# Windowed attention: the second image's statistics move into the attention loop, the first image's pieces load ahead of the bias table

## The chip, the cores and the metric

One core of a Trainium2 chip. The metric is the time of one execution on the device, in microseconds; three runs of the kernel before gave 3354.16, 3354.45 and 3354.75 us, median 3354.45 us.

## The reference

The input x is (2, 128, 128, 128): 2 images, 128 channels, 128 x 128 pixels, float32.

```
x = x + attention(group_norm(x))       # 8 heads of 16 channels in windows of 16 x 16 pixels, with a bias table
x = x + deformable(group_norm(x))      # DCNv4, 3 x 3 kernel, 8 groups
group_norm(v): 32 groups of 4 channels; mean and variance over 4 x 128 x 128 values of one image
attention: softmax(q k^T * scale + bias[relative position]) v, then a projection
```

The attention's group norm needs, per image, the mean and variance of every channel over 16384 pixels before the first window of that image can be normalised. The change touches only these statistics and what is loaded around them.

## The kernel before, in words

Everything is written out by hand: each engine has its own instruction stream, and semaphores are the only order between them. `attention` is followed by `deformable` (the second residual block), which takes about the second half of the time and is not touched.

SP issues every DMA of `attention`, in program order, on one queue. Before the loop over windows it issues: three weight loads; 16 copies of the bias table into `rel_rows` in DRAM (L301); 16 loads of 1 MB of x into the two buffers of `stats_in` (L307: 8 pieces of 2048 pixels for image 0, then 8 for image 1, each waiting until the piece two before it was used); 16 loads that spread the bias table over `nbias` (L314); 6 chunks of four image rows into `strips` (L318), each waiting for the chunk two before it.

DVE computes `bn_stats` on each piece in four parts of 512 pixels (L638), then `bn_aggr` (L641) and the chain `group_scales` (L135 to L157) with a matrix multiply on PE (L451) that sums channels of a group, and a square root on ACT (L567). It does so for image 0 and then for image 1. After that it waits for `bias_in` and negates `nbias` (L651), and adds the bias of v for the first pair (`read_v`, L661).

POOL waits for the scales of both images (`gn_ready`), and for the chunks of strips that hold the first two windows. For each pair of windows it then copies them out of `strips` (L406), normalises them (L414), and after PE (L457, L461) and ACT (L575, L580) have made q and k it splits them into three bfloat16 parts (`split`, L423 to L432).

The attention works on 64 pairs of windows, 32 for each image. A pair has 16 slots, one for each head of each of its two windows. In slot n: PE computes the scores (L479) into one of two PSUM banks, which is free again when DVE has read the slot two before; DVE adds the bias and takes the row maximum (`bias_max`, L674, two instructions with a register read each); ACT takes the exponential (L587); PE transposes the probabilities of slot n - 2 (L492); DVE copies odd slots' transposes (L683) and ACT even ones (L594); PE multiplies by v after each fourth slot (`weigh`, L507). At slot 7 and slot 15 DVE normalises one finished window (`norm`, L689 and L694), at slot 9 it reads v of the next pair (L661). All engines hold the loop over pairs as a first pair, a loop with two pairs in its body, and three last pairs.

In each pair SP issues: a clearing store to `far_sums` (L354); the strip chunk for six pairs on (L361); `restack`, 12 loads of 128 KB into `stack` for the next pair (L344), which are to land before PE's slot 0 of that pair; the stores of the finished windows (L349); and, when POOL has split the pair after the next, the store of its parts (L330), which `restack` of the next round reads back. SP waits in between for what each needs; its pair ends with the store of the window that DVE normalises at slot 15.

Of the kernel before, what the change touches and what calls it, by code (L numbers as in the profile page):

```python
# [14 lines left out]
B, C, H, W = 2, 128, 128, 128  # L15
PIX = H * W
P = 128
# [20 lines left out]
AHEAD = 2  # L38
GN_EPS = 1e-5
CHUNK = 4 * W  # L40

# [132 lines left out]
def attention(nc, x, w_qkv, b_qkv, bv_row, rel_rev, attended, rel_rows, parts_dram, info_out, far_sums):  # L174


    with ExitStack() as ctx:
# [59 lines left out]
        bias_in = sem("bias_in")  # L237
        bias_neg = sem("bias_neg")
# [53 lines left out]
        def _(sp):  # L292
# [4 lines left out]

            for xq in range(WS):
                src = bass.AP(rel_rev.tensor, rel_rev.offset + WS - 1 - xq, [[REL, NH * REL], [1, WS]])
                dst = rel_rows[xq].rearrange("(r k) -> r k", k=WS)  # L300
                sp.dma_start(dst, src).then_inc(rows_out, 16)  # L301
            for b in range(B):
                for n in range(NSTAT):
                    i = b * NSTAT + n
                    if i >= 2:
                        sp.wait_ge(st_used, count(i - 1))
                    sp.dma_start(stats_in[:, i % 2, :], x_chan[b][:, n * 2048:(n + 1) * 2048]) \  # L307
                      .then_inc(st_in[i % 2], 16)
# [6 lines left out]
            for n in range(6):  # L315
                if n >= 2:
                    sp.wait_ge(chunk_in[n % 2], count(16 * (n // 2)))
                sp.dma_start(strips[:, n * CHUNK:(n + 1) * CHUNK],  # L318
                             x_chan[0][:, n * CHUNK:(n + 1) * CHUNK]).then_inc(chunk_in[n % 2], 16)
# [68 lines left out]
        def _(pool):  # L388
# [45 lines left out]
            pool.wait_ge(gn_ready, count(2 * B))  # L434
# [4 lines left out]
            with pool.Fori(0, (PAIRS - 2) // 2) as i:  # L439
                for par in range(2):  # L440
                    normalise(2 * i + 2 + par, par)
                    split(2 * i + 2 + par)

        @block.tensor
        def _(pe):
# [3 lines left out]
            for b in range(B):  # L449
                pe.wait_ge(gn_step, count(3 * b + 3))  # L450
                nc.tensor.matmul(x_ps[:, 0:2], gmat[:], ex[:], start=True, stop=True).then_inc(gn_sum, 1)  # L451

# [99 lines left out]
            with pe.Fori(0, (PAIRS - 4) // 2) as i:  # L552
                pair(2 * i + 1, 1)
                pair(2 * i + 2, 0)
            pair(PAIRS - 3, 1)
# [8 lines left out]
        def _(act):  # L564
            for b in range(B):
                act.wait_ge(gn_ready, count(2 * b + 1))
                nc.scalar.activation(gv[:, 1:2], gv[:, 0:1], ACT.Sqrt).then_inc(gn_root, 1)  # L567
            act.wait_ge(weights_in, count(48))
# [51 lines left out]
            with act.Fori(0, (PAIRS - 4) // 2) as i:  # L620
                pair(2 * i + 1)
                pair(2 * i + 2)
            pair(PAIRS - 3)
# [8 lines left out]
        def _(dve):  # L632
            for b in range(B):
                for n in range(NSTAT):
                    i = b * NSTAT + n
                    dve.wait_ge(st_in[i % 2], count(16 * (i // 2 + 1)))
                    for m in range(4):
                        ins = nc.vector.bn_stats(bn[:, 4 * n + m, :], stats_in[:, i % 2, m * 512:(m + 1) * 512])  # L638
                    ins.then_inc(st_used, 1)
                dve.wait_ge(st_used, count(NSTAT * (b + 1)))  # L640
# [6 lines left out]
                group_scales(nc, dve, x_ps[:, 0:2], gst, gv, gn[:, b, 0:1], gn[:, b, 1:2], recip_done, 9 * b,  # L647
                             gn_ready, 2 * b, gn_root, b)
            RB = 9 * B
# [35 lines left out]
            def norm(win, w, par, k):  # L685
# [5 lines left out]
                dve.wait_ge(recip_done, count(RB + win + 1))  # L691
# [7 lines left out]
            def pair(p, par, first=False, left=AHEAD):  # L699
# [14 lines left out]
            with dve.Fori(0, (PAIRS - 4) // 2) as i:  # L714
                pair(2 * i + 1, 1)
                pair(2 * i + 2, 0)
# [918 lines left out]
```

## Time and profile before

| what | value |
|---|---|
| median of 3 runs | 3354.45 us |
| profiled execution, its own time | 3350.4 us |
| span of its trace (first to last instruction) | 3348.7 us |
| busy: PE, DVE, ACT, POOL | 81%, 81%, 56%, 33% of the span |
| first scores of the attention | 129 us from the span's start |
| end of the attention | about 1560 us |

"Busy" counts the instructions that an engine executes, not waits or DMA issues. In a timeline row the first number is the start, the second the time that the row covers, then come the engine, the line of the kernel and the operation; xN says that N instructions are merged, and the bracket at the end gives the idle time before the row and what ended it. SPq is SP's queue of DMA issues. The page's chain of waits covers the deformable half of the span, so the first half is read from timelines.

### The profile page before, as it was taken

The page shows a single profiled execution, that of the slowest core. Times are in us where ns is not written, and L with a number is a line of the kernel's source. Part 1 is how long each engine was busy: PE and PEld are TensorE (multiplying, and loading weights), DVE is VectorE, ACT ScalarE, POOL GpSimd, SP SyncE. Part 2 cuts the span into 40 slices and gives each one's busy share as a digit, 9 for nine tenths or more (in the row PEclk, how much of TensorE's full clock was granted, in tenths as well). Part 3 has the DMA queues.
Part 4 walks back from the last instruction along what each step waited for, and adds up shares of the span by engine and source line. Part 5 has one row for each costly group of instructions (what it writes and reads, how often), then busy time and mean ns, then how long its engine had stood idle before and what let it go on. Part 6 is the DMA issues. An engine that isn't in the chain of part 4 may idle for free.

```text
span 3348.7 us, 78453 instructions
## 1 busy us (share of the span) xinstructions
PE 2717.4 (81%) x22424; PEld 2178.8 (65%) x22424; DVE 2716.9 (81%) x6553; ACT 1882.3 (56%) x3529; POOL 1102.7 (33%) x1525
## 2 busy tenths in 40 slices
PE   0599999999999999995665999897856699989886
PEld 0355655565556655563555888887845598888885
DVE  5488888888888888885656999998945599999996
ACT  0488888888888888885262444442204544434420
POOL 0333333333333333332415322135421241115550
PEclk9999999999999999998898999998978899999998
DMA  6788888888888888885642333233365333333334
GB/s 221 126 142 140 146 136 142 139 144 137 143 139 147 136 142 138 141 143 109 199 138 84 99 97 98 93 99 88 89 242 160 110 118 94 96 96 98 105 91 161
DMA packets 350617, 432.47 MB, mean 129 GB/s; under 512 B 42224, under 2 KB 275072, under 8 KB 344304
## 3 DMA queue, kind: packets, MB, share of 16 engines
q1 hardware_dynamic: 338544, 423.85, 56.5%
q0 software_dynamic: 11904, 6.44, 1.6%
q8 instruction: 97, 1.59, 0.2%
q14 instruction: 72, 0.59, 0.1%
HBM read 283.33 MB, written 147.09 MB: 129 GB/s over the span
## 4 chain that ended last, share of the span: by engine, by line
DVE 19%; DMA 8%; issue 8%; PE 6%; POOL 6%; POOLq 2%; DVEq 1%; ACT 1%; SPq 1%; ACTq 0%
DVE prod L1536 11%; DVE tt L1520 2%; PE sum_ps L1297 2%; DMA vring<-vals 2%; DMA vals<-vring 2%; DMA vring<-attended 2%; DVE x L1547 2%; POOL gath L1113 2%; POOLq L1120 1%; PE wt_ps L1275 1%; DMA o_sel<-off_out,pos 1%; DVE my L1515 1%; PE sum_ps L1237 1%; POOL i_sel L1113 1%; PE om_ps L1260 1%
## 5 line engine op out<-in xcount | busy, mean ns | idle before, releaser
L587 ACT ACTIVATE prob<-sbias,nmax 128x256 f32<-128x256 f32 x2048 | 905.0, 501 | 196.1 <-DVE nmax L674 194.1
L1536 DVE TENSOR_TENSOR prod<-vring,wt_ps 128x1920 f32<-128x1920 f32 (+3 forms) x512 | 902.7, 1816 | 58.9 <-DMA vring<-vals 49.2
L674 DVE CUSTOM_DVE_ANT_0 sbias<-s_ps,nbias 128x256 f32<-128x256 f32 x2048 | 766.9, 421 | 224.3 <-PE s_ps L479 211.8
L1297 PE MATMUL sum_ps<-d_ident,prod 128*128 128x128 f32 x6400 | 758.7, 276 | 23.5 <-DVE prod L1536 23.5
L492 PE MATMUL pt_ps<-a_ident,prob 128*128 128x128 f32 x4096 | 644.3, 280 | 134.1 <-ACT prob L587 131.6
L1297 PEld LDWEIGHTS sum_ps<-d_ident,prod 128*128 128x128 f32 x6400 | 721.4, 143 | 38.4 <-DVE prod L1536 31.6
L492 PEld LDWEIGHTS pt_ps<-a_ident,prob 128*128 128x128 f32 x4096 | 447.3, 140 | 277.6 <-DVE probT L683 118.4
L479 PE MATMUL s_ps<-stack 96*128 96x256 bf16 x2048 | 396.2, 274 | 9.5 <-DMA stack<-parts_dram 9.5
L683 DVE COPY probT<-pt_ps 128x512 f32<-128x512 f32 x512 | 351.7, 687 | 11.8 <-PE pt_ps L492 11.7
L423 POOL CAST parts<-qk 128x1024 bf16<-128x1024 f32 x64 | 66.3, 1036 | 860.1 <-ACT qk L580 860.1
L1403 ACT COPY ssum<-sum_ps 128x512 f32<-128x512 f32 x64 | 37.5, 586 | 513.6 <-PE sum_ps L1307 513.6
L1275 PE MATMUL wt_ps<-tt,d_ident 128*128 128x144 f32 x2304 | 312.0, 291 | 0.0
L1275 PEld LDWEIGHTS wt_ps<-tt,d_ident 128*128 128x128 f32 x2304 | 306.9, 195 | 0.9
L479 PEld LDWEIGHTS s_ps<-stack 96*128 96x128 bf16 x2048 | 174.8, 98 | 203.5 <-issue 137.0
L594 ACT COPY probT<-pt_ps 128x512 f32<-128x512 f32 x512 | 290.2, 567 | 0.0
L507 PE MATMUL o_ps<-probT,va 128*32 128x256 f32 x4096 | 274.1, 385 | 0.9 <-DVE probT L683 0.9
L1128 POOL COPY first_e<-first_at 128x2 f32 x16 | 2.8, 178 | 784.3 <-issue 784.3
L1390 ACT ACTIVATE hat<-off,one_col 128x576 f32<-128x576 f32 x128 | 140.5, 1098 | 198.2 <-DVE tt L1520 198.2
L1520 DVE TENSOR_TENSOR tt<-hat,my 128x864 f32<-128x864 f32 x192 | 192.4, 1057 | 9.1 <-PE wt_ps L1275 0.5
L674 DVE DVE_READ_ACCUMULATOR2_ANT nmax<- 128x1 f32 x2048 | 170.8, 83 | 0.0
L1381 ACT COPY off<-om_ps 128x864 f32<-128x864 f32 x64 | 56.3, 880 | 202.6 <-PE om_ps L1260 184.9
L507 PEld LDWEIGHTS o_ps<-probT,va 128*32 128x32 f32 x4096 | 106.9, 109 | 87.8 <-issue 33.9
(166 smaller groups left out, 3489.9 us busy)
## 6 DMA issues: line engine op xcount, KB each, us to landing
stack<-parts_dram SPq DMA_DIRECT2D x768, 128.0 KB, 7.4
vring<-vals SPq DMA_DIRECT2D x270, 320.0 KB
parts_dram<-parts SPq DMA_DIRECT2D x64, 768.0 KB, 6.5
off_out<-off SPq DMA_DIRECT2D x64, 432.0 KB
strips<-x SPq DMA_DIRECT2D x68, 256.0 KB, 3.6
a_stats_in<-x SPq DMA_DIRECT2D x16, 1024.0 KB, 4.9
far_sums<-nothing SPq DMA_DIRECT2D x64, 256.0 KB, 2.1
attended<-on SPq DMA_DIRECT2D x256, 64.0 KB
```

The source lines that it names most:

```text
L479: mm = nc.tensor.matmul(s_ps[:, n % 2, half, :], stack[:, par, 0, h, at:at + P], stack[:, par, 1, h, w * NT:(w + 1) * NT], start=True, sto ...
L492: mm = nc.tensor.transpose(pt_ps[:, T_BANK[n % 4], kh, half * P:(half + 1) * P], prob[:, n % 4, half, kh * P:(kh + 1) * P], ident[:])
L507: mm = nc.tensor.matmul(o_ps[32 * j:32 * j + VA, t * NT:(t + 1) * NT], va[:, par, 2 * w + kh, 4 * t + j, :], probT[:, (4 * k + j) % 8, kh, ...
L587: ins = nc.scalar.activation(prob[:, n % 4, half, :], sbias[:, n % SBIAS, half, :], ACT.Exp, bias=nmax[:, n % SBIAS, half:half + 1], scale ...
L594: nc.scalar.copy(probT[:, n % 8], pt_ps[:, T_BANK[n % 4]]).then_inc(t_read_a, 1)
L674: ins = nc.vector.tensor_tensor_reduce(out=sbias[:, n % SBIAS, half, :], in0=s_ps[:, n % 2, half, :], in1=nbias[:, h, half, :], scale=1.0, ...
L683: nc.vector.tensor_copy(probT[:, n % 8], pt_ps[:, T_BANK[n % 4]]).then_inc(t_read_v, 1)
L1275: mm = nc.tensor.matmul(acc[:, :, jx:jx + KS, jy * G:(jy + KS) * G], ident[:], tt[:, jx, jy, 2 * half:2 * half + 2].rearrange("p r (a k) - ...
L1297: mm = nc.tensor.matmul(sum_ps[:, par, r * H:(r + 1) * H], prod[:, r % 2, dx, dy * C:(dy + 1) * C], ident[:], start=(r + dx + dy == 0), st ...
L1390: nc.scalar.activation(xy(hat[:, j]), xy_off(s), ACT.Abs, bias=0.0 if j == 1 else one_col[:, j // 2:j // 2 + 1]).then_inc(dist_ready, 1)
L1520: ins = nc.vector.tensor_tensor(tt[:, jx], hat[:, jx, :, 0:KG].unsqueeze(1) .to_broadcast([P, 3, COLS, KG]), my[:], ALU.mult)
L1536: nc.vector.tensor_tensor(prod[:, r % 2, first:last].rearrange("p a (t c) -> p (a t) c", c=CG), vring[:, at:at + wide].rearrange("p a (t c ...
```

## The change

SP issues pieces 0 and 1 of image 0 ahead of the 16 bias table transfers, pieces 2 to 7 behind them, then the six strip chunks, and only then the 16 `nbias` loads. The 8 pieces of image 1 are no longer loaded there. Instead image 1 is cut into 16 pieces of 1024 pixels (512 KB), one for each of the pairs 1 to 16: SP issues the load at the start of its pair, and DVE takes `bn_stats` of the two halves after `bias_max` of slot 10 and of slot 12. Behind pair 16, DVE, PE and ACT run the chain of aggregation, group sums, square root and scales for image 1, and a second loop does pairs 17 to 60. POOL waits for image 0's scales at its start and for image 1's before pair 32. The semaphore of the chain's steps is a new one (`gn_coef`) in place of `recip_done`, and PE waits on it before it uses the bank again.

```diff
+STAT_PAIRS = 16
+STAT_AT = 10
+STAT = PIX // STAT_PAIRS
...
+            def load_stats(n):
+                if n >= 2:
+                    sp.wait_ge(st_used, count(n - 1))
+                sp.dma_start(stats_in[:, n % 2, :], x_chan[0][:, n * 2048:(n + 1) * 2048]).then_inc(st_in[n % 2], 16)
+
+            for n in range(2):
+                load_stats(n)
             for xq in range(WS):
...
-            for b in range(B):
-                for n in range(NSTAT):
...
+            for n in range(2, NSTAT):
+                load_stats(n)
+            for n in range(6):
+                if n >= 2:
+                    sp.wait_ge(chunk_in[n % 2], count(16 * (n // 2)))
+                sp.dma_start(strips[:, n * CHUNK:(n + 1) * CHUNK],
+                             x_chan[0][:, n * CHUNK:(n + 1) * CHUNK]).then_inc(chunk_in[n % 2], 16)
             sp.wait_ge(rows_out, count(16 * WS))
             for yq in range(WS):
...
-            for n in range(6):
...
-            def pair(p, par, first=False, left=AHEAD):
+            def pair(p, par, first=False, left=AHEAD, piece=None):
+                if piece is not None:
+                    sp.wait_ge(st_used, count(NSTAT - 1 + piece))
+                    sp.sem_inc(sp_passed, 1)
+                    sp.dma_start(stats_in[:, 1 - par, 0:STAT],
+                                 bass.AP(x.tensor, x.offset + C * PIX + piece * STAT, [[PIX, P], [1, STAT]])) \
+                      .then_inc(st_in[1 - par], 16)
...
-            with sp.Fori(0, (PAIRS - 4) // 2) as i:
-                pair(2 * i + 1, 1)
-                pair(2 * i + 2, 0)
+            with sp.Fori(0, STAT_PAIRS // 2) as i:
+                pair(2 * i + 1, 1, piece=2 * i)
+                pair(2 * i + 2, 0, piece=2 * i + 1)
+            with sp.Fori(0, (PAIRS - 4 - STAT_PAIRS) // 2) as i:
+                pair(2 * i + STAT_PAIRS + 1, 1)
+                pair(2 * i + STAT_PAIRS + 2, 0)
...
-            pool.wait_ge(gn_ready, count(2 * B))
+            pool.wait_ge(gn_ready, count(2))
...
+            pool.wait_ge(gn_ready, count(4))
...
+            def group_sums(b):
                 pe.wait_ge(gn_step, count(3 * b + 3))
                 nc.tensor.matmul(x_ps[:, 0:2], gmat[:], ex[:], start=True, stop=True).then_inc(gn_sum, 1)
+                pe.wait_ge(gn_coef, count(9 * b + 1))
...
+            def stat_piece(par, piece, half):
+                if half == 0:
+                    dve.wait_ge(st_in[1 - par], count(16 * (NSTAT // 2 + 1) + 16 * ((piece - (1 - par)) // 2)))
+                ins = nc.vector.bn_stats(bn[:, bass.ds(2 * piece + half, 1), :].rearrange("p a b -> p (a b)"),
+                                         stats_in[:, 1 - par, half * 512:(half + 1) * 512])
+                if half == 1:
+                    ins.then_inc(st_used, 1)
...
                     bias_max(p, n)
+                    if piece is not None and n in (STAT_AT, STAT_AT + 2):
+                        stat_piece(par, piece, (n - STAT_AT) // 2)
...
+            with dve.Fori(0, STAT_PAIRS // 2) as i:
+                pair(2 * i + 1, 1, piece=2 * i)
+                pair(2 * i + 2, 0, piece=2 * i + 1)
+            dve.wait_ge(st_used, count(NSTAT + STAT_PAIRS))
+            scales(1)
+            with dve.Fori(0, (PAIRS - 4 - STAT_PAIRS) // 2) as i:
...
```

The loops of PE and ACT are split in the same place, with `group_sums(1)` and `root(1)` between the two halves.

## Rows read from the trace of the kernel before

**Rows 1.** The start, in order of time; last number in brackets: idle before.

```profile
5.12 10.85 SPq L301 DMA_DIRECT2D rel_rows<-rel  x16
16.03 22.59 SPq L307 DMA_DIRECT2D a_stats_in<-x  x7
20.95 4.92 DVE L638 BATCH_NORM_STATS2 a_bn<-a_stats_in 128x6 f32<-128x512 f32 x8 [20.95 <-DMA a_stats_in<-x]
...
40.94 31.56 SPq L307 DMA_DIRECT2D a_stats_in<-x  x9
43.18 5.00 DVE L638 BATCH_NORM_STATS2 a_bn<-a_stats_in 128x6 f32<-128x512 f32 x8 [2.26 <-DMA a_stats_in<-x]
48.21 1.02 DVE L641 BATCH_NORM_AGGREGATE a_mv<-a_bn 128x2 f32<-128x192 f32 x1
...
52.45 0.15 DVE L157 TENSOR_SCALAR a_gn<-a_gv 128x1 f32<-128x1 f32 x1
...
72.55 10.28 SPq L314 DMA_DIRECT2D nbias<-rel_rows  x16
...
82.87 12.64 SPq L318 DMA_DIRECT2D strips<-x  x6
...
91.49 2.29 DVE L651 TENSOR_SCALAR nbias<-nbias 128x4096 f32<-128x4096 f32 x1 [6.86 <-DMA nbias<-rel_rows]
95.41 0.61 POOL L406 COPY xraw<-strips 128x512 f32<-128x512 f32 x1 [87.38 <-DMA strips<-x]
...
117.46 1.28 ACT L587 ACT_TABLE_LOAD   x1
...
119.80 0.69 DVE L661 TENSOR_TENSOR va<-qkv_ps,bv_sb 128x512 f32<-128x512 f32 x1 [26.02 <-PE qkv_ps L467]
...
129.09 0.61 PE L479 MATMUL s_ps<-stack 96*128 96x256 bf16 x2 [9.53 <-DMA stack<-parts_dram]
```

**Rows 2.** Engines in a stretch of the loop: busy (instructions), granted clock, DMA share, GB/s.

```profile
130.00:600.00 470.00, 425.69 (x3760) 280.63 (x3759) 387.86 (x1658) 407.63 (x922) 163.75 (x147) 1.00 0.85 140
```

**Rows 3.** DMA issues of the first 130 us: KB each, median us to landing.

```profile
a_stats_in<-x SPq DMA_DIRECT2D x16, 1024.0 KB, 4.9
...
strips<-x SPq DMA_DIRECT2D x7, 256.0 KB, 2.8
```

**Rows 4.** Instructions on the statistics' input: ns min/median/max, first and last start.

```profile
L638 DVE BATCH_NORM_STATS2 a_bn<-a_stats_in x64: 675/678/695, 21.0 to 79.6; 128x6 f32<-128x512 f32 x64
```

**Rows 5.** One pair, DVE's slots 9, 15 and the next pair's slot 1.

```profile
611.88 0.43 DVE L674 CUSTOM_DVE_ANT_0 sbias<-s_ps,nbias 128x256 f32<-128x256 f32 x1 [0.72 <-PE s_ps L479]
...
619.38 0.42 DVE L674 CUSTOM_DVE_ANT_0 sbias<-s_ps,nbias 128x256 f32<-128x256 f32 x1 [0.72 <-PE s_ps L479]
...
622.71 0.42 DVE L674 CUSTOM_DVE_ANT_0 sbias<-s_ps,nbias 128x256 f32<-128x256 f32 x1 [0.43 <-PE s_ps L479]
```

**Rows 6.** The same pair on PE: transposes of slot 12, then the next pair's slot 0.

```profile
617.67 0.66 PE L492 MATMUL pt_ps<-a_ident,prob 128*128 128x128 f32 x4 [0.40 <-ACT prob L587]
...
620.61 0.39 PE L479 MATMUL s_ps<-stack 96*128 96x256 bf16 x2
```

**Rows 7.** SP's queue at the start of its next pair.

```profile
623.77 0.38 SPq L354 DMA_DIRECT2D far_sums<-nothing  x1
624.99 0.36 SPq L361 DMA_DIRECT2D strips<-x  x1
```

**Rows 8.** Single microseconds of that pair, columns as in rows 2.

```profile
617.00:618.00 1.00, 0.60 (x6) 0.33 (x4) 1.00 (x6) 1.00 (x4) 0.00 (x0) 1.00 1.27 125
618.00:619.00 1.00, 1.00 (x10) 0.67 (x7) 0.66 (x4) 1.00 (x4) 0.00 (x0) 1.00 1.04 330
...
621.00:622.00 1.00, 1.00 (x7) 0.57 (x5) 0.89 (x5) 0.57 (x2) 0.00 (x0) 1.00 0.00 0
```

**Rows 9.** Instruction fetches by DMA from 100 to 200 us: packets, MB, share.

```profile
q8 instruction: 4, 0.07, 0.4%
```

**Rows 10.** The same from 400 to 1500 us.

```profile
q8 instruction: 1, 0.02, 0.0%
```

More of the change, by code:

```diff
@@ L438, in _ @@
             split(1)
-            with pool.Fori(0, (PAIRS - 2) // 2) as i:
+            with pool.Fori(0, PAIRS // 4 - 1) as i:
                 for par in range(2):
@@ L442, in _ @@
                     split(2 * i + 2 + par)
+            pool.wait_ge(gn_ready, count(4))
+            with pool.Fori(0, PAIRS // 4) as i:
+                for par in range(2):
+                    normalise(2 * i + PAIRS // 2 + par, par)
+                    split(2 * i + PAIRS // 2 + par)
         @block.tensor
@@ L448, in _ @@
             pe.wait_ge(gmat_ready, count(3))
-            for b in range(B):
+            def group_sums(b):
                 pe.wait_ge(gn_step, count(3 * b + 3))
                 nc.tensor.matmul(x_ps[:, 0:2], gmat[:], ex[:], start=True, stop=True).then_inc(gn_sum, 1)
+                pe.wait_ge(gn_coef, count(9 * b + 1))
+            group_sums(0)
             def proj_q(p, par):
@@ L551, in _ @@
             pair(0, 0, first=True)
-            with pe.Fori(0, (PAIRS - 4) // 2) as i:
+            with pe.Fori(0, STAT_PAIRS // 2) as i:
                 pair(2 * i + 1, 1)
                 pair(2 * i + 2, 0)
+            group_sums(1)
+            with pe.Fori(0, (PAIRS - 4 - STAT_PAIRS) // 2) as i:
+                pair(2 * i + STAT_PAIRS + 1, 1)
+                pair(2 * i + STAT_PAIRS + 2, 0)
             pair(PAIRS - 3, 1)
@@ L564, in _, with root @@
         def _(act):
-            for b in range(B):
+            def root(b):
                 act.wait_ge(gn_ready, count(2 * b + 1))
                 nc.scalar.activation(gv[:, 1:2], gv[:, 0:1], ACT.Sqrt).then_inc(gn_root, 1)
+            root(0)
             act.wait_ge(weights_in, count(48))
@@ L619, in _ @@
             pair(0, first=True)
-            with act.Fori(0, (PAIRS - 4) // 2) as i:
+            with act.Fori(0, STAT_PAIRS // 2) as i:
                 pair(2 * i + 1)
                 pair(2 * i + 2)
+            root(1)
+            with act.Fori(0, (PAIRS - 4 - STAT_PAIRS) // 2) as i:
+                pair(2 * i + STAT_PAIRS + 1)
+                pair(2 * i + STAT_PAIRS + 2)
             pair(PAIRS - 3)
@@ L632, in _, with scales @@
         def _(dve):
[L633 to L640, printed above, removed]
+            def scales(b):
                 nc.vector.bn_aggr(mv[:], bn[:].rearrange("p a b -> p (a b)")).then_inc(gn_step, 1)
@@ L646, in _ @@
                 dve.wait_ge(gn_sum, count(b + 1))
-                group_scales(nc, dve, x_ps[:, 0:2], gst, gv, gn[:, b, 0:1], gn[:, b, 1:2], recip_done, 9 * b,
+                group_scales(nc, dve, x_ps[:, 0:2], gst, gv, gn[:, b, 0:1], gn[:, b, 1:2], gn_coef, 9 * b,
                              gn_ready, 2 * b, gn_root, b)
-            RB = 9 * B
+            for n in range(NSTAT):
+                dve.wait_ge(st_in[n % 2], count(16 * (n // 2 + 1)))
+                for m in range(4):
+                    ins = nc.vector.bn_stats(bn[:, 4 * n + m, :], stats_in[:, n % 2, m * 512:(m + 1) * 512])
+                ins.then_inc(st_used, 1)
+            dve.wait_ge(st_used, count(NSTAT))
+            scales(0)
             dve.wait_ge(bias_in, count(16 * WS))
@@ L690, in norm @@
                                      x_view[:, :, :, HD]).then_inc(recip_done, 1)
-                dve.wait_ge(recip_done, count(RB + win + 1))
+                dve.wait_ge(recip_done, count(win + 1))
                 dve.wait_ge(y_out[par], count(64 * k))
@@ L697, in norm, with pair @@
                                             .to_broadcast([P, NH, HD]), ALU.mult).then_inc(norm_done, 1)
-            def pair(p, par, first=False, left=AHEAD):
+            def stat_piece(par, piece, half):
[4 more added lines that the diff above has]
+                if half == 1:
+                    ins.then_inc(st_used, 1)
+            def pair(p, par, first=False, left=AHEAD, piece=None):
                 for n in range(SLOTS):
                     bias_max(p, n)
+                    if piece is not None and n in (STAT_AT, STAT_AT + 2):
+                        stat_piece(par, piece, (n - STAT_AT) // 2)
                     m = n - READ_LAG_V
@@ L713, in _ @@
             pair(0, 0, first=True)
-            with dve.Fori(0, (PAIRS - 4) // 2) as i:
-                pair(2 * i + 1, 1)
-                pair(2 * i + 2, 0)
+            with dve.Fori(0, STAT_PAIRS // 2) as i:
[4 more added lines that the diff above has]
+            with dve.Fori(0, (PAIRS - 4 - STAT_PAIRS) // 2) as i:
+                pair(2 * i + STAT_PAIRS + 1, 1)
+                pair(2 * i + STAT_PAIRS + 2, 0)
             pair(PAIRS - 3, 1)
```

10 lines of the change are left out of this document (1 added, 9 removed).

## The prediction

> **What bounds the kernel now.** I read the timeline of the start first, then the table of stretches, then single pairs of the loop. In the start the reader is to see one serial column up to the first scores at 129.09 us, in which almost nothing is computed [rows 1]. SP's queue sets it: 16 bias transfers from 5.12, sixteen 1 MB pieces from 16.03 to 72.5, sixteen `nbias` loads from 72.55, six strip chunks from 82.87. POOL can begin the first window only at 95.41, and the bracket there says on what: the strips, last in the queue. Scales of both images had been done 11 us earlier. From POOL's first copy to the first scores it takes 129.09 - 95.41 = 33.7 us (normalise, project, split, store, restack), and nothing of this depends on the statistics or on the bias.
>
> In the loop PE is nearest to full: 425.7 of 470 us, ACT 407.6, DVE 387.9, the 16 DMA engines at a share of 0.85 [rows 2]. But DVE's slack is not spread evenly. In the pair that I follow it waits 0.72 us for scores before slot 9 and 0.72 us before slot 15, and between these two rows, 7.5 us apart, the timeline shows no bracket at all: slot 9, the copy of a transpose, the read of v, then slots 10 to 14 one behind the other [rows 5]. In that run DVE sets the pace. PE waits inside it, 0.40 us for the exponential of slot 12 [rows 6]. The next pair has the same shape. So the change takes work from a stretch where it costs its full time and puts it into the one run of slots in which DVE has nothing to spare.
>
> **The start, step by step.** Pieces 0 and 1 are issued at 5.12, land some 4.9 us later [rows 3] and are used up by about 15, while SP still issues bias transfers. Two issues of 0.33 us (two issues of the 16 with no wait between them) put the bias transfers back to about 5.8, and their end from 16.0 to 16.7. Pieces 2 and 3 then stand where pieces 0 and 1 stood, 0.7 us later. A pair of pieces takes (43.18 - 20.95) / 3 = 7.41 us [rows 1], and image 0 now has three such pairs behind the bias transfers and not four. So its last `bn_stats` ends at 48.18 - 7.41 + 0.7 = 41.5, and the chain from aggregation to scales, 48.21 to 52.60 or 4.4 us, ends at 45.9.
>
> The strip chunks follow the last piece. Its issue at 40.94 moves to 40.94 - 7.41 + 0.7 = 34.2, it lands at 39.1, and the chunks behind it land two at a time, 2.8 us for each two [rows 3]: chunk 3, the last that POOL's first window needs, at about 43, chunk 5 at about 46. Scales at 45.9 are then what comes last, and POOL starts at 45.9 instead of 95.41: a gain of 49.5 us. If the chunks come 2 us later than I work out, it is 47.5; if the first pieces also shorten the three pairs by running into fewer bias packets, 51.
>
> What is late next: `nbias`. Its loads start when chunk 5 is issued, about 43.5. Before, from the first issue to the landing of the last it took 91.49 - 72.55 = 18.9 us, part of it behind a piece of x and two strips. That gives 62.4, and with the negation of 2.29 us, 64.7. DVE's next work, v of the first pair, moved from 119.80 to 70.3. There are 5.6 us to spare, so it costs nothing. SP is free of `nbias` issues at 54, long before the first parts are split (about 60.6), and the 2 MB have left the DMA queue by then or nearly so. The 33.7 us up to the first scores stay. The removed 32 `bn_stats` of image 1 lay inside the 49.5 and are not counted again.
>
> **The pieces in the loop.** Each of 16 pairs gets two `bn_stats` of 0.68 us [rows 4]; eight in a row take 5.00 us [rows 1], so one costs the queue behind it 0.62 us, and two 1.24. The one after slot 10 puts slots 11 and 12 off by 0.62, less a gap of 0.1 ahead of slot 12. The exponential of slot 12 was already what PE waited for at 617.67, so it moves that transpose by 0.5 to 0.6, and what stands behind it in PE's order: the scores of slot 15, the transposes of slot 13, `weigh`, the next pair's slot 0. The second piece puts slots 13 and 14 off by 1.1 in all. DVE's 0.72 us before slot 15 takes up most of that, and PE's transposes of slot 13, which need its exponential, come 0.7 late. After slot 15 PE, ACT and DVE are all 0.6 to 0.9 later than they were, and no engine has a slack of its own left to give it back. I take 0.65 us for a pair, 16 x 0.65 = 10.4 us. The ends: nothing, if PE's 10% of idle time [rows 2] takes it in after all; all of DVE's time, 16 x 1.24 = 19.8 us. A wait or a computed address on DVE's queue could add 0.2 us to each half, which the running instruction should hide; uncovered it is 6 us.
>
> `stat_piece` waits for its piece at slot 10. SP issues the load after the store of slot 15 of the pair before, some 10 us earlier, and a load of twice the size lands in 4.9 us: no wait. SP's own wait is for a piece used in the pair before the last: none.
>
> **The queue.** On SP the load adds an issue and an address ahead of the clearing store, the strip and the 12 loads of `stack`: between the starts of two such issues lie 1.22 us [rows 7]. On the DMA engines it adds 512 KB. `stack` is through at about 618.0, where the rate goes from 125 to 330 GB/s because the wide rows of the parts' store follow it [rows 8], and PE wants it at 620.61 [rows 6]: 2.6 us of slack, 3.2 with the 0.65 above. Two pieces of 1 MB in 7.41 us are 283 GB/s, so 512 KB take 1.85 us; all of it in front of `stack` makes 1.85 + 1.22 = 3.1 us, and part of it falls into the empty stretch at 621 [rows 8]. I take nothing, with little room. At the slow rate of 125 GB/s a piece would take 4.2 us, 5.4 with SP's part, 2.2 us beyond the slack in each pair, or 35 us in 16: the upper bound.
>
> The rule that would speak against the change here is in the Trainium skill, DMA: Bandwidth & Descriptors, section "Queues, rings and completion order": each DMA engine takes the descriptors of a queue in ring order. By it nothing of `stack` can pass the piece, and the whole 1.85 us count and not only what the gap leaves. The sum stays the same by either reading, since 3.1 is under 3.2, but by the rule the margin is a tenth of a microsecond.
>
> **The break behind pair 16.** DVE runs the chain alone, 4.4 us as at 48.21 to 52.60 [rows 1]; bias and maximum of the next slot 0 stand behind it. PE can issue the group sums, the two scores that have banks, the waiting transposes and a projection meanwhile, and then waits for slot 0's maximum. DVE's wait before slot 1 goes (0.43 us, rows 5), so 3.9 us are lost. ACT has to load the table for the square root and then that for the exponential, 1.28 us each [rows 1]: the first lies under the aggregation, the second under the reciprocal and what follows it. Ends: 3 us, if the matmuls done ahead give back more; 7, if a table load is exposed and PE, having paused, is slow for a few matmuls, as at 129.09 (0.61 us for two against 0.39 at 620.61, rows 1 and 6).
>
> POOL's second wait is met by pair 17, and POOL gets to it at pair 30: nothing. Everything after the attention only shifts.
>
> **Sum.** -49.5 + 10.4 + 0 + 3.9 = -35.2 us. Against the profiled execution's own 3350.4 us this is 3315.2; that execution was 4.05 us below the median of the runs, and on the median's footing it is 3319.3 us.
>
> **Rivals.** (a) The pieces are hidden in the loop: PE is the fuller engine over a pair and makes up the delay. For it: 10% idle on PE. Against: the waits inside the run of slots 9 to 14 are on the ring of DVE, ACT and PE. Sum -49.5 + 3.9 = -45.6, 3309 us. (b) DVE's added time counts in full, 19.8 us and some address work: -25.8 with the break, 3329 us. For it: the run without a bracket; against: the 0.72 us before slot 15. (c) The `stack` comes late: 35 us beside the 10.4, in sum 0, 3354 us. It sets in when the piece and SP's part together pass 3.2 us. For it: a DMA share of 0.85; against: an empty microsecond in each pair. (d) DVE's loop body no longer stays resident. One instruction packet of 16 KB was fetched between 400 and 1500 us [rows 10], so today the loops run without fetching. The body grows by four `bn_stats` with their waits and addresses, and there are now two loops on every engine. Four packets took 0.4% of 16 engines over 100 us, 1.6 us each [rows 9]. One such fetch exposed in each of the 8 + 22 iterations costs 48 us: +12.8, 3367 us, slower than before. It decides from 35.2 / 30 = 1.2 us for an iteration. Against: nothing in the trace says that the body is near any limit. A rule on it stands in the Trainium skill, Runtime: NRT & Kernel Launch, section "Instruction fetch mechanics": a taken branch whose target is outside the two blocks held stalls for the fetch. By it a body that straddles a third block pays in each iteration and one that doesn't pays nothing; the trace agrees with the second half only.
>
> **Chances.** Forecast 0.60 (its own range 3314 to 3326), (a) 0.15, (b) 0.15, (c) 0.04, (d) 0.06. 0.2% of this time, 6.7 us, is what can be told from no change. The first three are all faster: 0.90. (c) is no change, 0.04; (d) is slower, 0.06. The range is 3306 to 3334: from (a) with 51 us in the start to (b) with the break at 7.
>
> **What would show it.** POOL's first copy at 46 with gn or `strips` as its releaser; the first scores near 79.6; `nbias` negated before 66. In pairs 1 to 16 two `BATCH_NORM_STATS2` of 0.68 us with no wait on `a_stats_in`, and 16 pairs 10 us longer than 16 later ones. No wait of PE on `stack`. One hole of about 4 us behind pair 16. Wrong would be: `nbias` landing after 70, PE's waits for `stack`, or more than a few instruction packets between 250 and 1400 us.

## The result, and the profile after

The change makes the kernel slower: median 3364.6 us of 15 runs against 3354.75 us of 15 runs of the kernel before, ratio 1.003 with a 95% interval of 1.0021 to 1.0040. I forecast 3319.3 us. The profiled execution has a span of 3363.9 us, 15.2 us longer than before; the medians differ by 9.9 us, since the profiled execution of the kernel before was 4.4 us below its median.

To see where, I take one instruction that every pair has, POOL's first subtraction in `split`, and compare its start times in the timelines of both kernels (differences are of the unrounded times):

```
us                                           before    after   difference
first split from the span's start            104.4     61.8     -42.6
two pairs from there                          35.0     34.9      -0.1
the next 16 pairs                            357.7    364.5      +6.8
the pair with the break                       22.4     29.4      +7.0
the 44 pairs up to the last split            983.4   1019.9     +36.5
from the last split to the span's end       1846.0   1853.4      +7.5
```

The start gained most of what was forecast, and the 16 pairs with statistics cost less than forecast. What turned the sum is a line that I had at nothing: 44 pairs behind the break, in which the change does no work at all. Before, each pair there takes 22.4 us. After, pairs of 22.4 us and longer ones alternate; of the 21 longer ones eleven take 23.5 us and ten take 24.3 to 25.0 us.

The start, in order of time, answering to [rows 1]:

```profile
6.13 16.57 SPq L312 DMA_DIRECT2D rel_rows<-rel  x16
13.32 4.93 DVE L682 BATCH_NORM_STATS2 a_bn<-a_stats_in 128x6 f32<-128x512 f32 x8 [13.32 <-DMA a_stats_in<-x]
28.12 4.96 DVE L682 BATCH_NORM_STATS2 a_bn<-a_stats_in 128x6 f32<-128x512 f32 x8 [9.86 <-DMA a_stats_in<-x]
...
48.21 1.02 DVE L670 BATCH_NORM_AGGREGATE a_mv<-a_bn 128x2 f32<-128x192 f32 x1
...
52.82 0.61 POOL L422 COPY xraw<-strips 128x512 f32<-128x512 f32 x1 [44.70 <-DVE a_gn L160]
...
65.90 3.66 DVE L687 TENSOR_SCALAR nbias<-nbias 128x4096 f32<-128x4096 f32 x1 [13.30 <-DMA nbias<-rel_rows]
```

POOL starts on the scales, as forecast, but at 52.8 and not at 45.9. The aggregation begins at 48.21 us in both kernels. The bias transfers take SP 16.6 us to issue instead of 10.85, pieces 0 and 1 land at 13.3 us and later, not at 10, and behind the bias transfers DVE waits 9.86 us for piece 2. (In other kernels with the same order of issue this part was 2 to 3 us shorter: experiment 3.)

One turn of the second loop on ACT: the last work of one body, then the top of the next:

```profile
525.19 0.56 ACT L626 COPY probT<-pt_ps 128x512 f32<-128x512 f32 x1
526.89 1.28 ACT L619 ACT_TABLE_LOAD   x1 [1.13 <-DVE nmax L710]
528.18 1.71 ACT L619 ACTIVATE prob<-sbias,nmax 128x256 f32<-128x256 f32 x4
```

The load of the exponential's table comes behind the wait for slot 0's maximum, so nothing hides it. PE in the same place:

```profile
527.07 0.39 PE L504 MATMUL s_ps<-stack 96*128 96x256 bf16 x2
529.22 0.65 PE L517 MATMUL pt_ps<-a_ident,prob 128*128 128x128 f32 x4 [1.77 <-ACT prob L619]
529.71 0.47 PE L504 MATMUL s_ps<-stack 96*128 96x256 bf16 x2
530.02 1.11 PE L517 MATMUL pt_ps<-a_ident,prob 128*128 128x128 f32 x4
531.06 1.94 PE L532 MATMUL o_ps<-probT,va 128*32 128x256 f32 x16
```

And the stretch in steps of 2 us, columns as in [rows 2]:

```profile
528.00:530.00 2.00, 0.78 (x6) 0.58 (x6) 1.05 (x5) 1.99 (x6) 0.00 (x0) 0.97 0.46 165
530.00:532.00 2.00, 2.00 (x17) 1.20 (x20) 1.47 (x5) 2.00 (x5) 0.00 (x0) 0.50 0.69 187
532.00:534.00 2.00, 2.00 (x19) 1.07 (x12) 0.34 (x1) 1.01 (x3) 0.00 (x0) 0.68 0.96 133
```

PE stood idle for 1.77 us, and after that the granted clock is at the lower of its two levels, 1.2 GHz (0.50), for 3.4 us (0.03, 0.50 and 0.32 of three stretches of 2 us are missing from 1.00): four transposes take 1.11 us, not 0.60 to 0.66. In the loop of the kernel before it stays at 1.00 [rows 2].

The clock does not fall in every turn. Three turns later PE is idle as long, and the clock stays up (the last row is a stretch, as above):

```profile
669.33 0.65 PE L517 MATMUL pt_ps<-a_ident,prob 128*128 128x128 f32 x4 [1.75 <-ACT prob L619]
670.12 0.65 PE L517 MATMUL pt_ps<-a_ident,prob 128*128 128x128 f32 x4
670.00:672.00 2.00, 2.00 (x25) 1.05 (x24) 1.38 (x5) 2.00 (x5) 0.00 (x0) 1.00 0.65 174
```

It falls behind ten of the 21 table loads of this stretch, and these are the ten turns with the longest pairs. So the load alone costs 1.1 us a turn (23.5 against 22.4 us), and with the clock 2.4 us on average.

The table loads by line in the kernel after (count, busy us, mean ns, idle before):

```profile
L619 ACT ACT_TABLE_LOAD x23 | 29.5, 1283 | 26.1 <-DVE nmax L710 26.1
...
L597 ACT ACT_TABLE_LOAD x2 | 2.6, 1283 | 0.9 <-PEq L1680 0.9
```

23 loads on the exponential's line: one at 77.0 us, as the one of before, and 22, one in each turn of the second loop. The first of the 22 falls into the pair with the break, the other 21 into the 44 pairs.

### The profile page after: what moved, and what is told of

It is laid out like the page before. It is cut to its first block, busy times and chain, and to the rows that moved or that the text cites. A ratio compares the mean times of both kernels' runs of the same rounds, so it can differ in the third digit from the quotient of the medians.

```text
span 3363.9 us, 78405 instructions
## 1 busy us (share of the span) xinstructions
PE 2742.1 (82%) x22424; PEld 2196.5 (65%) x22424; DVE 2717.2 (81%) x6553; ACT 1907.7 (57%) x3552; POOL 1109.3 (33%) x1525
## 4 chain that ended last, share of the span: by engine, by line
DVE 21%; DMA 8%; issue 8%; PE 6%; POOL 5%; POOLq 2%; DVEq 1%; ACT 1%; SPq 1%; ACTq 0%
DVE prod L1587 13%; DVE tt L1571 3%; PE sum_ps L1348 2%; DMA vring<-vals 2%; DMA vals<-vring 2%; DVE x L1598 2%; PE wt_ps L1326 2%; DVE my L1566 1%; POOL gath L1164 1%; DMA o_sel<-off_out,pos 1%; POOLq L1171 1%; DMA x<-x 1%; PE om_ps L1311 1%; DVE vring L1511 1%; POOL i_sel L1164 1%
## 5 line engine op out<-in xcount | busy, mean ns | idle before, releaser
L719 DVE COPY probT<-pt_ps 128x512 f32<-128x512 f32 x512 | 351.6, 687 | 11.0 <-PE pt_ps L517 10.7
L1326 PE MATMUL wt_ps<-tt,d_ident 128*128 128x144 f32 x2304 | 323.5, 298 | 0.0
L1326 PEld LDWEIGHTS wt_ps<-tt,d_ident 128*128 128x128 f32 x2304 | 317.9, 201 | 7.9 <-issue 7.1
L532 PE MATMUL o_ps<-probT,va 128*32 128x256 f32 x4096 | 283.1, 395 | 0.9 <-DVE probT L719 0.9
L1571 DVE TENSOR_TENSOR tt<-hat,my 128x864 f32<-128x864 f32 x192 | 193.0, 1060 | 20.0 <-PE wt_ps L1326 10.5
```

Source lines behind the costliest of these rows:

```text
L532: mm = nc.tensor.matmul(o_ps[32 * j:32 * j + VA, t * NT:(t + 1) * NT], va[:, par, 2 * w + kh, 4 * t + j, :], probT[:, (4 * k + j) % 8, kh, ...
L719: nc.vector.tensor_copy(probT[:, n % 8], pt_ps[:, T_BANK[n % 4]]).then_inc(t_read_v, 1)
L1326: mm = nc.tensor.matmul(acc[:, :, jx:jx + KS, jy * G:(jy + KS) * G], ident[:], tt[:, jx, jy, 2 * half:2 * half + 2].rearrange("p r (a k) - ...
L1571: ins = nc.vector.tensor_tensor(tt[:, jx], hat[:, jx, :, 0:KG].unsqueeze(1) .to_broadcast([P, 3, COLS, KG]), my[:], ALU.mult)
```

## The experiments

**1. The table, from both sides.** Theory T: the 36.5 us are table loads on the path, one in each turn, with what PE's clock loses to them. `exp_first` is the changed kernel with one more line behind the square root, writing to a tile that nobody reads:

```diff
             root(1)
+            nc.scalar.activation(warm[:], bqn_sb[:], ACT.Exp)
```

> The changed kernel with one throwaway exponential of 128 values on ACT, right behind the square root of image 1. Theory T (table): in the changed kernel ACT loads the exponential's table anew in each of the 22 iterations of the second loop (23 loads on the exponential's line, 1.28 us each), because the loop is entered with the square root's table and comes round with the exponential's; a pair of pairs there takes 46.6 us against 44.75 before. Then the 22 loads shrink to one ahead of the loop, and the time falls by 22 x 1.85 = 40 us, to about 3325, below the kernel before. Rival C (code): the second loop is slow because splitting the loops moved the code; then nothing changes, 3364. Rival Q (queue): it is an after-effect of the DMA order; nothing changes either.

`table_only` is the kernel before, ACT's stream alone touched:

```diff
-            with act.Fori(0, (PAIRS - 4) // 2) as i:
+            with act.Fori(0, 8) as i:
...
+            nc.scalar.activation(warm[:], gv[:, 1:2], ACT.Sqrt)
+            with act.Fori(0, (PAIRS - 4) // 2 - 8) as i:
```

> The kernel before, with none of the change, except that ACT's loop is split after 8 iterations and one throwaway square root of 128 values stands between the two. Theory T: 22 table loads appear, and the kernel is 22 x 1.85 us plus one load slower than before, about 3355 + 42 = 3397. Rivals C and Q: no statistics, no new order of loads, no split on the other engines, so the time stays at 3355 (C allows a few us for ACT's code alone).

Measured: `exp_first` 3331.1 us, 0.9922 of before (0.9908 to 0.9935); `table_only` 3403.2 us, 1.0143 (1.0127 to 1.0158). The 44 last pairs take 983.6 us in `exp_first`, where they took 983.4 before the change, and 1023.6 in `table_only`. Table loads of `exp_first`, then of `table_only`:

```profile
L598 ACT ACT_TABLE_LOAD x2 | 2.6, 1283 | 0.9 <-PEq L1682 0.9
...
L620 ACT ACT_TABLE_LOAD x1 | 1.3, 1283 | 0.0
L657 ACT ACT_TABLE_LOAD x1 | 1.3, 1283 | 0.0
```

```profile
L588 ACT ACT_TABLE_LOAD x23 | 29.5, 1283 | 24.1 <-DVE nmax L679 24.1
```

T stands, C and Q fall as causes of this stretch: a throwaway square root between two loops costs the kernel before 47 us, and a throwaway exponential takes some 34 us off the changed one. I had expected 42 and 40. Of the 47 us the 44 pairs explain 40 and the pair with the square root 1.5; the rest no stretch of the trace shows, and its profiled execution was itself 9 us below its median. A load of 1.28 us costs 36.5 / 21 = 1.74 us in the changed kernel, 40.2 / 21 = 1.91 us in `table_only`, where the clock fell behind 12 of the 21.

**2. What a statistic costs in a pair.** Both are `exp_first` with one thing changed. `slots_8_14`:

```diff
-                    if piece is not None and n in (STAT_AT, STAT_AT + 2):
-                        stat_piece(par, piece, (n - STAT_AT) // 2)
+                    if piece is not None and n in (8, 14):
+                        stat_piece(par, piece, (n - 8) // 6)
```

> exp_first with the two halves of a piece taken behind slots 8 and 14, ahead of the two slots before which DVE waits 0.72 us for scores, instead of behind 10 and 12 in the run without a gap. If a statistic costs what DVE's slack at its place leaves over, the 0.45 us that a pair of the first loop takes longer (22.8 against 22.35) fall to under 0.1, and 16 pairs save 5 to 7 us against exp_first. If what costs is the piece's load on the queues, the place makes no difference.

`no_bn`, in `stat_piece`:

```diff
-                ins = nc.vector.bn_stats(bn[:, bass.ds(2 * piece + half, 1), :].rearrange("p a b -> p (a b)"),
-                                         stats_in[:, 1 - par, half * 512:(half + 1) * 512])
                 if half == 1:
-                    ins.then_inc(st_used, 1)
+                    dve.sem_inc(st_used, 1)
```

> exp_first with the bn_stats of image 1 left out in the loop (image 1 is normalised with image 0's statistics); the loads of its pieces and all waits stay. If DVE's work is what the first loop's pairs pay for, they fall from 22.8 to 22.4 us and the kernel saves 7 us against exp_first. If SP's issue or the DMA engines are, nothing changes.

Measured: 3321.3 us (0.9899; 0.9884 to 0.9915) and 3320.9 us (0.9898; 0.9882 to 0.9913). The 16 pairs take 364.5 us in `exp_first`, 358.5 in `slots_8_14`, 358.1 in `no_bn`, 357.7 before. So it is DVE's time in the run of slots 9 to 14 that costs, 0.43 us a pair; ahead of a slot for which DVE waits anyway the same instruction costs 0.05 us a pair, and the pieces' loads cost nothing that shows. The medians fall by 10, of which this accounts for 6 and a break shorter by 1.3 us for some more; the intervals of `exp_first` and of these two overlap, so the rest may be scatter of the runs.

**3. The start.** `pieces_behind` is `slots_8_14` with the two early loads back in their old place, and `bias_on_act` is `slots_8_14` with L312 and L325 issued by ACT:

```diff
-            for n in range(2):
-                load_stats(n)
             for xq in range(WS):
...
-            for n in range(2, NSTAT):
+            for n in range(NSTAT):
```

> slots_8_14 with pieces 0 and 1 of image 0 issued behind the 16 bias transfers again, as in the kernel before. My prediction gave the early issue 7.4 - 0.7 = 6.7 us, so this would be 6.7 us slower, 3328. Theory S (SP stalls): the 2 MB in front of the small transfers make SP's 16 issues take 16.6 us instead of 10.9 and the pieces land at 13.3, so the last bn_stats of image 0 ends at 48.2 us either way; then the time stays at 3321, within 1.5 us.

```diff
-                sp.dma_start(dst, src).then_inc(rows_out, 16)
+                act.dma_start(dst, src).then_inc(rows_out, 16)
...
-                sp.dma_start(nbias[row * WS:(row + 1) * WS, :, half, :], src).then_inc(bias_in, 16)
+                act.dma_start(nbias[row * WS:(row + 1) * WS, :, half, :], src).then_inc(bias_in, 16)
```

> slots_8_14 with the 16 bias transfers and the 16 nbias loads issued by ACT, which is idle until 51 us, and all pieces of image 0 and the strips by SP from 5 us on. If SP's queue is what the first scales wait for, they come 16.6 us (the stretch of bias issues on SP) less some sharing of the DMA engines earlier: last bn_stats at about 37, POOL's first copy at about 42 instead of 52.8, and the kernel gains about 10 us, 3311. If the DMA engines are what the pieces wait for (4304 small packets beside them), it gains under 3 us.

Measured: `pieces_behind` 3324.8 us (0.9911; 0.9896 to 0.9927), by the medians not told apart from `slots_8_14`. The traces do tell them apart; its own:

```profile
5.19 10.87 SPq L311 DMA_DIRECT2D rel_rows<-rel  x16
16.09 25.23 SPq L306 DMA_DIRECT2D a_stats_in<-x  x8
...
48.26 1.02 DVE L670 BATCH_NORM_AGGREGATE a_mv<-a_bn 128x2 f32<-128x192 f32 x1
```

The same of `slots_8_14`, from which it differs in nothing else:

```profile
6.13 14.39 SPq L313 DMA_DIRECT2D rel_rows<-rel  x16
45.29 1.02 DVE L672 BATCH_NORM_AGGREGATE a_mv<-a_bn 128x2 f32<-128x192 f32 x1
```

With the bias transfers first they are issued in 10.87 us again, and the aggregation begins 3.0 us later, at 48.26 and not at 45.29. The other kernels bear this out. The first aggregation begins at 45.3 to 45.9 us in seven kernels that issue the pieces early and load the bias by SP, with 14.4 to 14.7 us for the bias issues, and at 48.1 to 49.4 us in the six that issue them behind. The changed kernel's own profiled execution, with 16.57 and 48.21, is the one exception; one trace does not say why. So the early issue brings some 2.5 to 3 us, less than half of the 6.7 us that I gave it: with 2 MB in front of the small transfers, SP takes 3.5 us longer to issue them. `bias_on_act` is worse, 3331.8 us (0.993; 0.9915 to 0.9946):

```profile
0.87 15.78 ACTq L593 DMA_DIRECT2D rel_rows<-rel  x16
...
38.54 2.47 DVE L684 BATCH_NORM_STATS2 a_bn<-a_stats_in 128x6 f32<-128x512 f32 x4 [6.78 <-DMA a_stats_in<-x]
...
50.77 2.47 DVE L684 BATCH_NORM_STATS2 a_bn<-a_stats_in 128x6 f32<-128x512 f32 x4 [5.39 <-DMA a_stats_in<-x]
```

Pieces 2 and 3 come earlier, but the `nbias` loads, issued by ACT from 21.0 to 32.3 us, then run beside the later ones, and the aggregation begins at 53.27 us, 8.0 us later than in `slots_8_14`. The DMA engines' share is 1.04 to 1.11 from 25 to 45 us, against 0.64 to 0.95 there, so they were what was short. I had expected a gain of 10 us, or of under 3; against `slots_8_14` it was a loss of 10.5.

`order_only` is the kernel before with only SP's order of the change: two pieces first, all 16 MB of statistics still in the start, strips ahead of `nbias`.

```diff
+            for i in range(2):
+                load_stats(i)
             for xq in range(WS):
...
+            for i in range(2, B * NSTAT):
+                load_stats(i)
+            for n in range(6):
...
             sp.wait_ge(rows_out, count(16 * WS))
             for yq in range(WS):
```

> The kernel before with only SP's order changed as in the changed kernel: pieces 0 and 1 ahead of the bias transfers, the six strip chunks ahead of the nbias loads; the statistics of image 1 stay in the start. POOL then waits for the scales of image 1 and not for the strips: it starts at 84.9 us instead of 95.4 and the kernel gains 10.5 us, 3346. Of the 42.6 us that the changed kernel's start gained, the moved statistics then account for the other 32. If nbias, now last, holds DVE up beyond the v of the first pair (due at 109 us; I expect it negated at 103 to 106), it gains less.

Measured: 3339.9 us, 0.9956 (0.9942 to 0.9969), 15.8 us below the kernel before, where I had expected 10.5. (The profiled execution was 9.4 us above that median.)

```profile
82.44 0.61 POOL L410 COPY xraw<-strips 128x512 f32<-128x512 f32 x1 [74.40 <-DVE a_gn L157]
...
98.94 2.29 DVE L655 TENSOR_SCALAR nbias<-nbias 128x4096 f32<-128x4096 f32 x1 [16.70 <-DMA nbias<-rel_rows]
106.85 0.69 DVE L665 TENSOR_TENSOR va<-qkv_ps,bv_sb 128x512 f32<-128x512 f32 x1 [5.62 <-PE qkv_ps L471]
```

POOL starts 13.0 us earlier than before: 2.4 us of it are the early pieces (image 1's aggregation begins at 77.89, not at 80.29), the rest the order of strips and `nbias`. So of the 42.6 us about 13 are the order of issue and 30 are the moved statistics. The first scores come 10.7 us earlier, at 118.37 us; the rest of the 15.8 us this trace does not show. `nbias`, now last, is negated 5.6 us before DVE has its next work.

**4. The deformable part.** From the last split to the end it is 7.5 us longer in the profile after, and 9 to 12 us in `exp_first`, `slots_8_14` and `no_bn`. In its loop over groups PE waits for nothing that the profile shows, once per image; the row of before, of `slots_8_14` and of `pe195` (total, times, longest):

```profile
PE wt_ps L1270 <- issue: 5.7, 2, 2.9
```

```profile
PE wt_ps L1323 <- issue: 14.2, 2, 7.2
```

```profile
PE wt_ps L1326 <- issue: 5.2, 2, 2.7
```

Instruction fetches lie in these stops. Packets of them in the long stop of `slots_8_14` (2065.5 to 2073 us) and in the short one of `pe195` (2078 to 2081 us):

```profile
q8 instruction: 2, 0.03, 1.6%
```

```profile
q8 instruction: 1, 0.02, 2.0%
```

The theory was that the loops' copy in the attention moved the later code. Idle semaphore increments move it back, or move that of before:

```diff
+            for _ in range(N):
+                act.sem_inc(filler, 1)
```

with N = 197 behind ACT's attention (`before_pad`) and 59 there (`pad_act`); the same on PE's start with 61 (`before_pe61`), 829 (`before_pe829`) and 195 (`pe195`); `pe195_act59` has 195 on PE's and 59 on ACT's start. `pad_act`, `pe195` and `pe195_act59` build on `slots_8_14`, the others on the kernel before.

> The kernel before with 197 idle semaphore increments on ACT behind its attention part, where ACT has some 60 us of nothing to do: they move ACT's code of the deformable part by as many instructions as the changed kernel with the throwaway exponential moves it. Theory P (place of the code): the 8 to 12 us by which the deformable part is longer in every kernel with the change come from ACT fetching instructions at another place in its loop (idle for 'issue' on ACT in that part 20.9 us against 6.8 + 2.2 before). Then this kernel is 5 to 12 us slower than before, all of it behind 1510 us. Rival R: the deformable part is longer for another reason (DMA, clock, PE's or DVE's code); then nothing changes, 3355.

> slots_8_14 with 59 such increments on ACT, so that ACT's deformable code has moved by 256 instructions in all against the kernel before. Theory P: its fetches fall where they fell before, and the deformable part gets 5 to 10 us shorter, 3311 to 3316 against 3321. If place doesn't count or another engine's does, 3321.

> The kernel before with 61 idle semaphore increments at the start of PE's program, where PE waits 49 us for the first statistics. PE's code grew by 829 instructions in the changed kernel, 61 more than three times 256; so this puts PE's deformable code where the change puts it, modulo 256. Theory P2 (PE's place): PE stands still for 'issue' once per image for 7 us instead of 2.9 (13.8 against 5.7 us in all), and the deformable part gets 4 to 12 us longer: 3360 to 3368 against 3356. If the place of PE's code isn't it, 3356.

> slots_8_14 with 195 such increments at PE's start, so that PE's code in the deformable part has moved by four times 256 against the kernel before. Theory P2: PE's 7 us stops go back to 2.9 and the kernel gains 4 to 10 us, 3311 to 3317 against 3321. Otherwise 3321.

> pe195 with 59 increments at ACT's start as well, where ACT waits 51 us. ACT's stops for issue in the deformable part (20.9 us in slots_8_14) vanished with the shift in pad_act without a gain, since PE's stop was the longer one. If they count once PE's are short, 1 to 4 us below pe195; else the same.

> The kernel before with 829 idle increments at PE's start, the whole number by which the change makes PE's code longer, and not that number less three times 256. They must fit into the 49 us in which PE waits for the first statistics; if they don't, the first group sum comes after 50.3 us and the excess is to be taken off. Theory P3 (place counts, but not modulo 256 instructions): PE's stops in the deformable part go from 2.9 to 7 us per image and the kernel is 4 to 10 us slower, 3360 to 3366. Rival (not the place, but something that the loop split or the statistics leave behind): 3356, and the 7 us stops stay unexplained.

Measured:

```
               us      ratio                       PE's stops, us in all
before_pad     3364.5  1.0029 (1.0018 to 1.0040)    5.6
pad_act        3321.4  0.9898 (0.9885 to 0.9911)   13.8
before_pe61    3354.8  1.0002 (0.9993 to 1.0011)    5.9
pe195          3315.5  0.9879 (0.9864 to 0.9894)    5.2
pe195_act59    3318.3  0.9892 (0.9876 to 0.9907)    5.4
before_pe829   3432.8  1.0222 (1.0202 to 1.0241)    6.6
```

ACT's place is not it: its fillers took its stops away in both kernels, and the changed one gained nothing. (These stops, of ACT in its loop over groups, also come and go where its code has not moved: 6.8 us before, 25.0 us in `order_only`.) (`before_pad` lost 8 us. Its fillers run from 1557.9 to 1571.4 us, and the deformable part's first work on DVE comes at 1598.5 instead of 1590.5, which fits their own time.)

For PE the medians alone don't decide: that of `pe195` is 5.8 us lower than that of `slots_8_14`, with intervals that overlap, and 61 or 829 fillers gave the kernel before no long stop. (829 were too many to hide: PE's first group sum came at 128.5 us instead of 49.7, which is most of the loss; its profiled execution was besides 12.8 us above its median.) The time up to the second image, however, scatters between kernels by up to 12 us, with no pattern that follows the change. From the second image's first product on DVE (the 257th `prod<-vring`) to the end of the span there is one:

```
us                                                          second image    longest stop of PE
before, order_only, table_only, before_pad, before_pe61     707.8 to 708.6    2.8 to 3.2
before_pe829                                                710.4             3.4
after, exp_first, slots_8_14, pieces_behind                 714.6 to 715.2    6.9 to 7.2
no_bn, pad_act, bias_on_act                                 712.7 to 713.1    6.7 to 7.2
pe195, pe195_act59                                          708.9, 707.7      2.7, 2.9
```

The change makes the second image 4 to 7 us longer, with two fetch packets one behind the other in PE's long stop where there was one, and 195 instructions ahead of PE's code take both away, in two kernels. In the first image the long stop stands too (its fifth group takes 91 us, not 86), but the first group is some 5 us shorter, 106.5 against 112.1 us before, and the two cancel. So a shift of PE's code alone takes the long stop away. That the shift alone put it there is not shown: 61 and 829, meant to give the kernel before the changed kernel's place, did not. This part stays open.

## Why the prediction was wrong

**The step that failed** is in "The break behind pair 16". I put the loads of both tables there, "the first lies under the aggregation, the second under the reciprocal and what follows it", and then gave the second loop nothing. The count was wrong: not one load of the exponential's table but 22. Not even the first lay where I put it: it stands behind the wait for slot 0's maximum, not under the reciprocal.

```profile
479.46 1.28 ACT L619 ACT_TABLE_LOAD   x1 [2.44 <-DVE nmax L710]
```

Before, a pair stands ahead of the loop, so the loop is entered with the exponential's table and comes round with it, and [rows 1] has the only load, at 117.46. Behind `root(1)` the second loop is entered with the square root's table and comes round with the exponential's, and the load is placed in the body, good for both ways in. The price in the trace is 36.5 us for 21 of the loads, and up to 1.9 us for the first, by which the pair with the break is longer than in `exp_first`; `exp_first` and `table_only` show it from both sides. The Trainium skill, ScalarE activation tables: per-element evaluation and per-set limits, section "Table sets in the compiler and the runtime", says that table loads are placed block by block. The trace agrees, if a loop's body is such a block: the body got a load of its own. Read beside the split loop, that sentence would have pointed at the 22 loads, though not at their price.

**Where it was hidden.** I asked of a table load only whether the break covers it, and not in which loop it would stand. Rival (d), slower by something that each turn of a loop pays, with its point of decision at 1.2 us a turn, had the right shape and nearly the price, 1.74 us in a turn of the second loop; its cause, code that no longer stays resident, was the wrong one. Between 400 and 600 us 8 fetch packets came (4 on q8, the queue of [rows 10], and 4 on q14), and none from 600 to 1500.

**The start**: forecast 49.5, measured 42.6. The order of what is late was right (scales, not strips; `nbias` with slack). The 6.7 us for the early pieces were not: I left SP's issue time of the bias transfers at 10.85 us whatever stands in front of them, and it became 16.6 in this execution, 14.4 to 14.7 in seven other kernels with the same order. In those the pieces gave 2.5 to 3 us: POOL starts at 49.90 us in `slots_8_14`, a gain of 45.5. `nbias` was negated at 65.9, forecast 64.7, but in 3.66 us and not in 2.29, and POOL's copy beside it took 2.67 instead of 0.61; the two first pairs together lost nothing by it that shows.

**The pieces in the loop**: forecast 10.4, measured 6.8, with the mechanism that I gave: no wait for a piece, none of PE for `stack` after the first, and the cost gone once the statistics stand elsewhere. I gave PE too much of the added time, 0.65 us a pair where it was 0.43; which of the two pieces it was no run separates. The margin of a tenth of a microsecond on the queue was not used up.

**The break**: forecast 3.9; 7.0 after, of which the table load of the first turn is a part, and 5.1 in `exp_first`:

```profile
475.26 0.61 PE L505 MATMUL s_ps<-stack 96*128 96x256 bf16 x2 [0.55 <-DVE a_gv L140]
475.66 1.06 PE L518 MATMUL pt_ps<-a_ident,prob 128*128 128x128 f32 x4
476.51 1.88 PE L483 MATMUL qkv_ps<-xn,wqkv_sb 128*128 128x512 f32 x2
478.22 0.39 PE L505 MATMUL s_ps<-stack 96*128 96x256 bf16 x2
```

PE waited 2.1 us for the group sums, and its next matmuls took almost twice their time (0.61 for 0.39, 1.88 for 1.02), with the granted clock at 0.50 from 476 to 478 us. Four other kernels with the throwaway exponential have the same, and 27.2 to 27.5 us for the pair. In `slots_8_14`, `no_bn` and `pe195` the clock stays at 1.00 in the break and the pair takes 26.2 us, 3.8 more than before. So the 3.9 us were right where the clock held, and the upper end of 7 was right for what happened in the changed kernel.

**After the attention** I wrote that everything only shifts. It did not: 7.5 us in the profile, of which the second image's 7.4 us follow PE's code, as above.

Summed for the profiled execution: -42.6 - 0.1 + 6.8 + 7.0 + 36.5 + 7.5 = +15.1 us, and the spans differ by 15.2. Without the 36.5 it would have been a gain of 21 us.

The lowest median is that of `pe195`, 3315.5 us, 1.2% below the kernel before: the change, one throwaway exponential, the statistics at slots 8 and 14, and the fillers. Without them `slots_8_14` has 3321.3, and the intervals of the two overlap.

## What to carry to other kernels

Before a function of another table goes into or between loops, look at which table each loop is entered with and with which it comes round; where they differ, the load is in the body and is paid in each turn, and one throwaway activation ahead of the loop removes it. Price an added instruction by the wait that follows it in its engine's order, not by the engine's mean slack: 1.24 us of DVE cost 0.43 us a pair in a run without gaps and nearly nothing ahead of two slots with a 0.72 us wait. Large loads ahead of many small transfers on one queue can hold back the engine that issues them. And read no difference of a few microseconds from one trace: the changed kernel's first aggregation came 2 to 3 us later in its trace than in those of seven kernels with the same order of issue.

## What the runs showed of the hardware that I had not expected

A pause of 1.75 us on PE, in a loop that kept it 90% busy, was followed by 3.4 us at half the clock in ten of 21 turns and by full clock in the other eleven, so a table load of 1.28 us cost 1.1 us in some turns and 2.4 in others, 1.74 on average. 829 semaphore increments in a row on PE took 128.5 us, 0.155 us each; 197 on ACT took 13.5 us, 0.07 us each. A POOL instruction that started while DVE's negation of `nbias` ran ended only behind it: a copy took 2.67 us instead of 0.61 in the changed kernel and in `slots_8_14`, and one of 128x2 values 2.26 us instead of 0.18 in `pe195`. The negation took 3.66 us and not 2.29 in the changed kernel, where it began beside a subtraction of POOL. PE's stop for instructions in the deformable part took 2.6 to 3.4 us with one fetch packet of 16 KB and 6.6 to 7.2 us with two.
